# Issuing two small transfers per batch from ScalarE's queue instead of SyncE's

## What is computed

```
x = x + tanh(g_xattn) * (softmax(mask(LN(x) Wq . ctx Wk) / 4) ctx Wv) Wo      (+ biases)
x = x + tanh(g_ffn)   * tanh(((LN(x) W1) W2) W3 + bias)
```

## Time and profile before

| | |
|---|---|
| median of three runs | 1095.0 us |
| time of the profiled execution | 1093.47 us |
| span of its trace | 1091.3 us |
| granted TensorE clock, mean | 0.989 |
| TensorE matmul busy | 1043.5 us, 96% |
| VectorE busy | 907.2 us, 83% |
| ScalarE busy | 823.4 us, 75% |
| GpSimd busy | 773.7 us, 71% |
| chain that ended last, by engine | PE 90%, DVE 5%, SP's queue 2%, DMA 2% |
| L281, the moved transfers | 256 issues of 4 KB on SP's queue |

### The profile page before, as it was taken

The page is one execution under the profiler, slowest core; times in us unless marked ns, Lnnn a source line. Parts: engine busy times, 40 slices in busy tenths (PEclk is TensorE's granted clock), DMA queues, the critical chain, the costliest instruction groups (busy, mean ns, idle before and its releaser), DMA issues.

```text
span 1091.3 us, 45222 instructions
## 1 busy us (share of the span) xinstructions
PE 1043.5 (96%) x18723; PEld 913.9 (84%) x18723; DVE 907.2 (83%) x1272; ACT 823.4 (75%) x1275; POOL 773.7 (71%) x1184
## 2 busy tenths in 40 slices
PE   5988999999999999999999999999999999999965
PEld 4777888888888888888888888888888888888855
DVE  5778888888888888888888888888888888888766
ACT  4566887787787787778778778777877877877742
POOL 5255787787777778778777777877877777777653
PEclk9999999999999999999999999999999999999987
DMA  6134334434434433443444453444344344343232
GB/s 162 44 95 123 102 110 139 114 112 134 133 106 122 142 107 113 141 114 114 132 119 120 121 143 109 110 141 114 114 132 132 105 123 136 110 115 113 85 121 69
DMA packets 180158, 127.92 MB, mean 117 GB/s; under 512 B 109809, under 2 KB 146930, under 8 KB 179954
## 3 DMA queue, kind: packets, MB, share of 16 engines
q1 hardware_dynamic: 179810, 124.77, 40.1%
q10 hardware_dynamic: 144, 0.26, 0.1%
HBM read 70.46 MB, written 53.48 MB: 114 GB/s over the span
## 4 chain that ended last, share of the span: by engine, by line
PE 90%; DVE 5%; SPq 2%; issue 2%; DMA 2%; ACT 0%; DVEq 0%
PE ps_m L475 17%; PE ps_m L468 17%; PE ps_s L568 13%; PE ps_s L589 13%; PE ps_x L600 11%; PE ps_m L530 9%; PE ps_m L462 6%; PE ps_s L574 4%; DVE neg_max L949 2%; DVE probs L960 2%; DMA a_rows<-scratch_a 0%; DMA den<-a_den 0%; DMA scratch_m<-max_T 0%; SPq L204 0%; PE ps_m L613 0%
## 5 line engine op out<-in xcount | busy, mean ns | idle before, releaser
L949 DVE TENSOR_REDUCE neg_max<-ps_s 128x16 f32<-128x2048 f32 x128 | 293.2, 2291 | 81.0 <-PE ps_s L574 81.0
L960 DVE TENSOR_TENSOR probs<-ps_s,far_T 128x2048 f32<-128x2048 f32 x128 | 293.3, 2291 | 15.5 <-PE ps_s L589 9.7
L760 ACT ACTIVATE probs<-probs 128x2048 f32<-128x2048 f32 x128 | 244.5, 1910 | 8.2 <-DVE probs L960 7.9
L735 ACT ACTIVATE q_aug<-ps_m,q_bias,q_scale 128x256 f32<-128x256 f32 x256 | 123.4, 563 | 159.3 <-PE ps_m L468 150.8
L409 POOL TENSOR_TENSOR y<-y,th 128x512 f32<-128x512 f32 x58 | 73.9, 1275 | 160.7 <-ACT th L781 122.2
L568 PE MATMUL ps_s<-k_aug,q_aug 32*128 32x128 f32 x4096 | 150.7, 283 | 16.7 <-DVE probs L960 8.2
L568 PEld LDWEIGHTS ps_s<-k_aug,q_aug 32*128 32x128 f32 x4096 | 128.1, 186 | 39.2 <-issue 31.3
L589 PE MATMUL ps_s<-q_aug,k_aug 32*128 32x128 f32 x4096 | 151.4, 283 | 4.1 <-DVE neg_max L949 2.3
L589 PEld LDWEIGHTS ps_s<-q_aug,k_aug 32*128 32x128 f32 x4096 | 127.1, 186 | 21.8 <-issue 4.2
L600 PE MATMUL ps_x<-probs,v_ones 128*32 128x128 f32 x4096 | 139.8, 278 | 4.1 <-issue 2.8
L600 PEld LDWEIGHTS ps_x<-probs,v_ones 128*32 128x32 f32 x4096 | 105.2, 110 | 33.2 <-issue 33.2
(11 more groups left out here) (120 smaller groups left out, 1720.3 us busy)
## 6 DMA issues: line engine op xcount, KB each, us to landing
scratch_a<-a_den SPq DMA_DIRECT2D x64, 512.0 KB, 3.1
x_in<-in_x SPq DMA_DIRECT2D x64, 256.0 KB, 3.5
a_rows<-scratch_a SPq DMA_DIRECT2D x64, 256.0 KB
den_wide<-scratch_r SPq DMA_DIRECT2D x64, 256.0 KB
out<-y SPq DMA_DIRECT2D x64, 256.0 KB, 4.9
ctx_in<-in_ctx SPq DMA_DIRECT2D x252, 64.0 KB, 3.4
q_aug<-scratch_m SPq DMA_DIRECT2D x256, 4.0 KB
scratch_m<-max_T SPq DMA_DIRECT2D x128, 16.0 KB
```

What stands on the lines that cost most here:

```text
L735: last = nc.scalar.activation(dst[:, :, 2 * m + a, :], src[:, m * TOK:(m + 1) * TOK].rearrange("p (n q) -> p n q", q=P), ACT.Identity, bia ...
L760: nc.scalar.activation(tile, tile, ACT.Exp).then_inc(probs_ready, 1)
L949: nc.vector.tensor_reduce(neg_max[:, 0:H].rearrange("p (j c) -> p j c", j=G), ps_s[:], AX.X, ALU.max, negate=True).then_inc(max_ready, 1)
L960: nc.vector.tensor_tensor(probs[i % 2][:].rearrange("p j s q -> p (j s) q"), ps_s[:].rearrange("p j s q -> p (j s) q"), far_T[:].unsqueeze ...
```

## The change

`read_max` is taken out of SyncE's program and put, with the same waits, transfers and counts, into ScalarE's. `read_max(2t)` stands behind `spread_q(t+1)` and ahead of `exponents(2t-1)`. `read_max(2t+1)` stands behind `high_of_ctx(t+2)` and ahead of `keep_f(t-5)` and `high_of_x(t+2)`.

```diff
@@ sync
-            def read_max(i):
-                sp.wait_ge(max_stored[i % 2], 16 * (i // 2 + 1))
-                heads = scratch_m[i % 2][0:H].rearrange("(j m a) q -> a j m q", j=G, a=2)
-                for a in range(2):
-                    slots = q_aug[i // 2 % 2][D * (1 - a)::ROWS, i % 2].rearrange("p (m a) q -> p a m q", a=2)
-                    sp.dma_start(slots[:, a], heads[a]).then_inc(max_landed[i % 2], 16)
...
                 if is_pair(t + 4):
                     load_x(t + 4)
-                read_max(2 * t)
                 write_max(2 * t + 1)
                 if is_pair(t - 2):
                     write_reciprocals(t - 2)
                     read_a(t - 2)
-                read_max(2 * t + 1)
                 if is_pair(t - 2):
                     read_wide(t - 2)
@@ scalar
+            def read_max(i):
+                act.wait_ge(max_stored[i % 2], 16 * (i // 2 + 1))
+                heads = scratch_m[i % 2][0:H].rearrange("(j m a) q -> a j m q", j=G, a=2)
+                for a in range(2):
+                    slots = q_aug[i // 2 % 2][D * (1 - a)::ROWS, i % 2].rearrange("p (m a) q -> p a m q", a=2)
+                    nc.scalar.dma_start(slots[:, a], heads[a]).then_inc(max_landed[i % 2], 16)
...
                 if is_pair(t + 1):
                     spread_q(t + 1)
+                read_max(2 * t)
                 if is_batch(2 * t - 1):
                     exponents(2 * t - 1)
...
                 if is_pair(t + 2):
                     high_of_ctx(t + 2)
+                read_max(2 * t + 1)
                 if is_pair(t - 5) and t - 5 < END:
                     keep_f(t - 5)
                 if is_pair(t + 2):
                     high_of_x(t + 2)
```

## The result

The changed kernel takes 1120.35 us, the median of 4 runs (1114.59 to 1125.39), against 1095.21 (1094.87 to 1095.8) for the kernel before: a ratio of 1.0227, interval 1.0174 to 1.028. That is 25 us slower, where 8.5 were forecast. The profiled execution of the changed kernel took 1114.59 us, with a span of 1112.5 against 1091.3 before. The changed kernel measured a second time took 1115.15 (experiment 5), so some 19 to 25 us is what it costs.

What follows compares the result with a forecast made beforehand. TensorE was taken to bound the middle (matmuls busy 99%), SP's queue and transfers the tail. 1093.5 + 8.0 + 1.5 - 1.0 = 1102.0, plus 1.5 from profiled run to median: 1103.5 us; range 1093.5 to 1138.

Steps and rivals of the forecast that it cites:

- likeliest case: Middle: a stall of 0.05 to 0.25 us a turn, 1097.3 to 1109 us; chance 0.48.
- queues that exclude each other: Odd half: `read_wide` slips between ScalarE's two issues, 0.60 us a turn, 1138 us; chance 0.08, shared with half the even pairs showing.
- even pairs that show: Even half: late pairs delay the exponents 0.6 us in half the turns, 17 us; chance 0.08, shared with queues excluding each other.
- When the maxima land: Middle: pairs issued as before or about a microsecond later, read by `scores_T` over 5 us later; no new wait.
- tail: After the middle: `read_den` issued about 1 us earlier without the odd pair ahead of it, -1.0 us, bounds 0 and -3.
- th and xT held: Odd half: th and xT 0.24 us late, `scores_T` 0.14 late after slack, 57 turns: +8.0 us, bounds 0 and +56.
- late landings of the write: Odd half: ScalarE holds `keep_f` 0.48 us more for a late write, three turns: +1.5 us, bounds 0 and +5.
- SP's queue in the middle: Middle: transfers that move up feed GpSimd, later turns or the maxima's own way; TensorE waits for none: 0.
- landing of the odd pair: Odd half: issued at the same time as before, so no new wait of `scores_T`: 0.
- even pair: Even half: a 1.13 us issue hides under four activations of 1.93 us behind `spread_q`: 0, upper bound 17 us.
- stand still: Both halves: ScalarE stops computing while its queue issues, 1158 or 1202 us; rival, chance 0.13.

Runs made afterwards that it cites:

- experiment 5: The changed kernel measured once more, unaltered, as the reference for the runs beside it: 1115.15 us, ratio 1.0171.
- experiment 1, Experiment 1: Kernel before with only the even batch's pair of reads issued by ScalarE, the odd pair staying on SP: 1105.12 us, ratio 1.0075.
- experiment 8: Kernel before, everything on SP, with the odd pair issued behind `read_wide` instead of ahead of it: 1103.63 us, ratio 1.0069.
- experiment 7: Changed kernel with the odd pair moved behind `high_of_x` on ScalarE instead of ahead of `keep_f`: 1175.81 us, ratio 1.0721.
- experiment 6: Kernel before with only the odd pair on ScalarE, and SP's `read_wide` waiting until `keep_f` is done: 1112.6 us, ratio 1.015.
- experiment 4: Kernel before with the real odd pair on ScalarE and an unread copy issued by SP in its old place: 1123.55 us, ratio 1.0239.
- experiment 3: Kernel before with the real odd pair on SP, plus an unread copy issued by ScalarE at the change's place: 1121.15 us, ratio 1.0221.
- Experiment 2: Kernel before with only the odd pair issued by ScalarE, the even pair staying on SP: 1126.28 us, ratio 1.0264.

## Why the prediction was off

The direction and the first mechanism were right. The size was not, 25.1 us against 8.5 in the medians and 21.2 against 8.5 in the profiled executions. The measured time lies in the stated range of 1093.5 to 1138, but outside that of the likeliest case, 1097.3 to 1109. What reached that far up were two rivals, queues that exclude each other and even pairs that show, and neither happened: that the range held is luck. The step that failed is "When the maxima land": "No new wait there". By its terms:

| term | predicted, us | measured, us |
|---|---|---|
| tail | -1.0 | -0.8 (47.35 against 48.16), not separable from the clock |
| th and xT held, with late landings of the write | 8.0 + 1.5 | A, 11.1, and 0.75 in t = 0 |
| SP's queue in the middle, landing of the odd pair | 0 and 0 | B, 6.7, and 2.0 in t = 2 and 4 |
| even pair | 0 | 0.5, late in 1 turn of 57 |
| not placed, the 0.5 of the even pair within it | | 1.5 |

*The tail.* `read_den` went 1 us earlier, as said, and its 3.98 us until use were not shorter but 4.15. The -0.8 is close to the forecast, but that is no proof: experiment 1, with the pair still on SP, had a tail of 46.90. By the Trainium skill ("DMA: Bandwidth & Descriptors", Issuing engines are not separate DMA queues), transfers that different engines start run on the same 16 DMA engines and interleave. What the trace of the tail shows agrees: the read was issued earlier and its data came no sooner behind the issue. The prediction cited that page for the tail alone. Its other half, the interleaving, speaks against the change in the middle, and it was not weighed there.

*The even pair* was right, with its condition. The prediction said that the pair hides if SP's queue gets shorter and costs up to 17 us if it doesn't. Experiment 1 is the second case, with 6.8 us in 11 turns instead of the 29 turns of 0.6 that the bound took.

*th and xT.* In an ordinary turn the forecast nearly stands: th 0.21 later instead of 0.24, and `scores_T` 0.10 late (7.59 against 7.49) instead of 0.14. What was too small is the number of late landings of the write. Three turns were assumed; in 14 of 56 the pair was issued over 2.15 behind the write, and these turns hold 5.8 of the 11.1 us. They brought th to 3.24 in the mean. The evidence was in the trace before: 17 of the same 56 odd reads on SP were issued over 2.15 behind the write. I read the earlier trace rows as one turn's exception and did not count how many there were. The row needs a count over all turns, not one example.

*The landing.* Two errors made it a zero. The lesser one: the margin was read from the start of the pair's issue (521.03 - 515.51, over 5 us), where 4.4 us count, from its end; of these about 0.9 were to spare in the old order (experiment 8). The one that cost the time: "what moves up feeds GpSimd, later turns" asked who *waits* for the transfers that move up, not whom they travel beside. Before, the pair was ahead of `read_wide`, the store and the context's loads in one queue. Now these start as early as 0.18 us behind it (510.30 against 510.12 above), or 0.27 (526.60 against 526.33). In the change the pair is issued as early as before, and in the turn at 605.63 its data still came 4.95 us after the end of its issue, where 3.85 had been enough before (experiment 7). Experiments 6 and 4 take the waits away by putting SP's transfers back behind a pair. Experiment 8 brings them about with the order alone, without ScalarE, though part of its wait is that the read is 0.83 later.

The packets show it directly. ScalarE's reads are the only transfers of the turn in queue q10 of the trace, 24 packets a pair (SP's are in q1), so one can see when a pair's last packet comes. In the changed kernel, t = 5 to 60, it comes 2.31 to 4.42 us behind the end of the issue, 3.76 in the median, in the 50 turns in which `read_wide` is issued within 0.2 us of the pair's start. In the other six, where `read_wide` happens to be 0.78 us or more behind, it comes after 1.69 to 2.17 us. In experiment 6, which holds `read_wide` back in every turn, it comes after 1.50 to 2.12. Here are the packets of q10 (packets, MB, share) from 530.5 to 531.3 us in the changed kernel, 3.1 to 3.9 us behind an issue that ended at 527.38, and from 560.0 to 561.5 us in experiment 6, 0.7 to 2.2 us behind one that ended at 559.34:

```profile
q10 hardware_dynamic: 12, 0.00, 2.2%
q10 hardware_dynamic: 24, 0.01, 2.1%
```

Half of the first pair's packets are still on their way when all of the second's have long come. That the transfers let loose on SP are the cause is shown by this and by experiments 6 and 4, and a head start of some 0.8 us over them is enough. It is not a place behind them in one queue, since the queues are different. Which of them does it is open: `read_wide`, the store and the loads always moved together.

*The rivals.* ScalarE does not stand still (518.64 beside 518.63, exponents on time). The queues do not exclude each other for a whole issue: in the rows above ACTq's pair takes 1.10 us with SP's 0.61 inside it, and no 0.60 is added. There is a smaller effect of that kind, though. With two transfers issued by both queues at once the pair went from 1.08 to 1.26 us (experiment 3), which at a stall of one to one is 0.18 a turn. The Trainium skill's rule on a generator locked for exclusive use ("Perfetto Trace Analysis", DMA Instruction — HWDGE (DVE, Sync)), taken to hold for the whole recorded issue as the prediction took it, would have made it 0.60 a turn; the runs show less than a third of that.

*What stays open.* Experiment 2, with less moved, is slower than the full change (1126 against 1115 to 1120; they ran on different chips). Some 4 us of that are the gap between its two issues in every fourth turn; where the gap and the rest come from is open. So is how the extra 0.19 us of th in experiment 3 splits between the longer issue and its second wait, and the 1.5 us that no part holds.

## What to carry to other kernels

Moving a small transfer off a queue also lets everything behind it go earlier: ask not only who waits for what moves up, but which urgent transfer it now travels beside, and measure that one's margin from the end of its issue. A margin read in the old order (about 0.9 us here) says nothing about the new one. An issue on a computing engine's queue is free only while activations already handed over run on *and* its own wait is over; whatever follows it on the queue inherits the jitter of what it waits for. So count, over all turns, how late the awaited event comes before the change. An idle queue (SP) absorbs that jitter for nothing, and here this was worth more than the microseconds that its issues take.

## What the runs showed of the hardware

- A transfer pair on ScalarE's queue takes about what it takes on SP's: 506, 514 and 1095 ns (lowest, median, highest) for one issue against 498, 526 and 706, and activations handed over before run on beside it.
- A read of two times 4 KB had its last packet 1.50 to 2.12 us behind the end of its issue when the larger transfers of the other queue were issued behind it (experiment 6), and 2.31 to 4.42 when one of 256 KB was issued within 0.2 us of its start. The scores could use it without a wait 3.85 us behind the end of the issue in one case (243.27 in the kernel before), and had to wait until 4.57 us (531.95 - 527.38) and 4.95 in two others.
- When two queues issue pairs at the same moment, ScalarE's takes 1.26 us instead of 1.08. They don't exclude each other.
- From the last write of maxima to the end, the twelve traces took 46.2 to 50.1 us, at mean granted clocks of 0.92 to 0.75 in that stretch, though their programs differ little there.
